# A graph layer with a routed feed-forward: the router's additions, the slots' owners and how the experts get their rows

## The reference, cut to what matters

```python
xn = layernorm(x)
x = x + relu(gcn(xn, edges, W) + b) + mix(xn)          # gcn: sum over edges of h[src] / sqrt(deg[src] deg[dst])
h = layernorm(x)
probs = softmax(h @ gate_w + gate_b)                     # 8 experts
idx = argmax(probs); prb = probs[idx]
pos = (number of earlier nodes with the same idx)
kept = pos < 977
buf[idx, pos] = h where kept
hmid = relu(buf @ w1 + b1)                               # 977 x 256 x 1024 per expert
ybuf = hmid @ w2 + b2                                    # 977 x 1024 x 256 per expert
x = x + nan_to_num(ybuf[idx, min(pos, 976)] * (prb * kept))   # nan -> 0, +-inf -> +-10000
```

## Time and profile before

| | us |
|---|---|
| median of three runs | 3071.05 (3069.43 to 3091.04) |
| the profiled execution, its own time | 3054.78 |
| its span, first to last instruction | 3053.0 |
| `prepare` | 0 to 166.5 |
| `aggregate_and_mix` | 166.5 to 2515.6 |
| `route` | 2515.6 to 2633.2 |
| `experts` | 2633.2 to 3053.0 |

### The profile page before, as it was taken

How to read it: one execution, slowest core, us unless ns; L and a number is a source line. 1 busy time by engine, 2 the same in 40 slices (tenths; PEclk the granted TensorE clock), 3 DMA queues, 4 the chain that set the end, 5 groups by cost and what they waited for, 6 DMA issues and landing times. The chain is left out here.

```text
span 3053.0 us, 35559 instructions
## 1 busy us (share of the span) xinstructions
PE 1786.6 (59%) x8925; PEld 1543.9 (51%) x8925; DVE 1245.6 (41%) x3349; ACT 813.4 (27%) x1591; POOL 1787.7 (59%) x1892
## 2 busy tenths in 40 slices
PE   2746556646555555655555555556433336599997
PEld 2634444445455444554455444545432335488986
DVE  3522222223333433433434334343322229478885
ACT  1312122212222222222232222222200006445452
POOL 6046556666666666666666666666666654244545
PEclk6878788866666666666666676666566565699998
DMA  5367766666666666666666655666566653322120
GB/s 172 141 198 220 213 201 190 178 187 185 185 186 184 176 180 185 178 174 177 179 186 188 181 172 171 182 181 177 170 188 183 181 164 121 119 68 96 57 97 11
DMA packets 194891, 502.10 MB, mean 164 GB/s; under 512 B 35250, under 2 KB 76225, under 8 KB 194586
## 3 DMA queue, kind: packets, MB, share of 16 engines
q0 software_dynamic: 132160, 423.59, 47.8%
q1 hardware_dynamic: 62554, 76.36, 7.6%
HBM read 461.89 MB, written 41.92 MB: 165 GB/s over the span
## 5 line engine op out<-in xcount | busy, mean ns | idle before, releaser
L767 POOL DMA_INDIRECT ring<-node_rows,src_chunk x1563 | 1486.3, 951 | 920.2 <-issue 434.2
L805 PE MATMUL p_item<-ring,sel 128*128 x3512 | 847.0, 393 | 647.6 <-DVE acc L1051 371.8
L805 PEld LDWEIGHTS p_item<-ring,sel 128*128 128x128 f32 x3512 | 690.9, 275 | 747.3 <-issue 744.8
L1051 DVE TENSOR_TENSOR acc<-acc,p_item 128x256 f32 (+1 forms) x439 | 183.6, 418 | 628.2 <-remote 495.0
L1033 DVE SCALAR_TENSOR_TENSOR sel<-dst_chunk,nbase,p_col 128x512 fp32r<-128x512 f32 x439 | 325.7, 742 | 62.3 <-issue 50.8
L845 PE MATMUL p_g<-x1T,w1t_sb 128*128 128x128 f32 x392 | 100.5, 437 | 206.6 <-ACT x1T L958 171.5
L845 PEld LDWEIGHTS p_g<-x1T,w1t_sb 128*128 128x128 f32 x392 | 86.3, 324 | 220.4 <-ACT x1T L958 181.9
L1056 DVE SCALAR_TENSOR_TENSOR kf<-p_q,ke 128x256 f32<-128x256 f32 x49 | 20.8, 425 | 404.3 <-ACT ke L991 348.7
L1561 POOL TENSOR_TENSOR low<-low,big 128x256 f32<-128x256 f32 x64 | 56.6, 885 | 172.5 <-DVE big L1741 172.0
L1675 PE MATMUL e_y<-w2h,hTh 128*128 128x256 f32 x512 | 148.8, 291 | 2.2 <-DVE hTl L1727 1.6
L1675 PE MATMUL e_y<-w2h,hTl 128*128 128x256 f32 x512 | 143.0, 279 | 0.0
(11 more groups left out here) (242 smaller groups left out, 3165.1 us busy)
## 6 DMA issues: line engine op xcount, KB each, us to landing
ring<-node_rows,src_chunk POOLq DMA_INDIRECT x1563
self_rows<-node_rows SPq DMA_DIRECT2D x49, 256.0 KB
node_rows<-halves SPq DMA_DIRECT2D x11, 1024.0 KB, 4.3
w1raw<-in_w SPq DMA_DIRECT2D x8, 1024.0 KB, 7.0
w2raw<-in_w SPq DMA_DIRECT2D x8, 1024.0 KB, 6.0
expert_rows<-empty SPq DMA_DIRECT2D x61, 130.0 KB
rows<-expert_rows SPq DMA_DIRECT2D x8, 910.0 KB
res<-in_x SPq DMA_DIRECT2D x7, 896.0 KB, 7.4
```

The lines of the kernel that those rows point to most:

```text
L767: nc.gpsimd.indirect_dma_start(ring[:, c % RING // U, c % U, :], None, table, bass.IndirectOffsetOnAxis(src_chunk[:, c:c + 1], 0)).then_in ...
L805: mm = pe.matmul(p_item[i % PSLOT][:, 0:C], sel[:, i % SELR, u, :], rows[:, u, h * C:(h + 1) * C].bitcast(F32R), start=(u == 0 and h == 0) ...
L1051: nc.vector.tensor_tensor(a, a, p_item[j % PSLOT][:, 0:C], ALU.add).then_inc(added, 1)
```

## The change

In `aggregate_and_mix` the writes of zeros are gone. The block's bias is now added when the node's own row is copied into `acc`, multiplied by `sqd` = sqrt(deg), and three operations at the end of the mixing work take the factor `sqd` as well, so that `acc` and `res` have one scale; the number of operations stays as it was, the three and the copy being other forms. `sqd` is one more operation at the end of `prepare`.

In `route` one addition per block is left in `x2`. PE transposes the rows as they are, the gate's weights are centred once instead, and the logits are scaled. The groups are 12, 12, 12, 8 and 5 blocks, and the small operations stand among the blocks of the next group. Instead of a row number for a scatter, each node gets a slot number, split into `slot_lo` (0 to 127) and `slot_hi` (0 to 63). DVE makes one-hot matrices of them (`one_hi`, `one_lo`, `node_of`), and PE sums them over all nodes to the node of each slot (`owners`). SP writes the rows with their columns to `node_features`; ACT multiplies the rows by `dinv` for the output.

In `experts` POOL gathers an expert's rows from `node_features` with eight indirect DMAs of 128 rows: those of experts 0 and 1 at the start, those of expert e+2 behind the last store of expert e. POOL's addition of `rows` is gone; DVE adds them behind its choice of finite numbers, and `total` is gone. Before its addition DVE waits until the store of the tile before the last has read `oo`. ACT waits for all eight gathers of an expert, for the first expert tile by tile.

```diff
-SLOTS = EXP * CAP
-NFILL = -(-SLOTS // P)
...
-RGR = 7
-NOUT = NBLK // RGR
+RB = [0, 12, 24, 36, 44, NBLK]
+RGM = 12
+NOUT = 2 * (len(RB) - 1)
...
-                if k >= 20 and k % 4 == 0 and (k - 20) // 4 < NFILL:
-                    lo = (k - 20) // 4 * P
-                    rows = min(P, SLOTS - lo)
-                    sp.dma_start(slots[lo:lo + rows, :], empty[0:rows, :]).then_inc(dma_empty, 16)
...
-                nc.vector.tensor_copy(acc[:, b, 0:C], p_self).then_inc(self_out, 1)
+                nc.vector.scalar_tensor_tensor(acc[:, b, 0:C], g["bias_b"]["gb"][:], sqd[:, b:b + 1], p_self,
+                                               ALU.mult, ALU.add).then_inc(self_out, 1)
...
-                    nc.vector.tensor_tensor(yn[:], yn[:], g["bias_b"]["ln2g"][:], ALU.mult).then_inc(fin, 1)
+                    nc.vector.scalar_tensor_tensor(yn[:], yn[:], sqd[:, b:b + 1], g["bias_b"]["ln2g"][:], ALU.mult,
+                                                   ALU.mult).then_inc(fin, 1)
...
-                    V.scalar_tensor_tensor(acc[:, b, 0:C], acc[:, b, 0:C], dinv[:, b:b + 1], g["bias_b"]["gb"][:],
-                                           ALU.mult, ALU.add).then_inc(s1, 1)
-                for b in range(gi * GR, gi * GR + GR):
-                    v.wait_ge(s1, b + 1)
-                    V.scalar_tensor_tensor(acc[:, b, 0:C], acc[:, b, 0:C], 0.0, res[:, b, :], ALU.max, ALU.add
-                                           ).then_inc(s2, 1)
...
+            def x2(b):
+
+                V.scalar_tensor_tensor(acc[:, b, 0:C], acc[:, b, 0:C], 0.0, res[:, b, :], ALU.max, ALU.add
+                                       ).then_inc(x2_ok, 1)
+
+            def stats(gi, b):
+                v.wait_ge(x2_ok, b + 1)
+                chain(V.bn_stats(stt[:, gi % 2, b - RB[gi], :], acc[:, b, 0:C]))
...
+                if i == 2:
+                    chained()
+                    chain(V.scalar_tensor_tensor(slot[:, 0:k], m2[:, 0:k], float(RT * P), place[:, 0:k], ALU.mult,
+                                                 ALU.add))
+                    chain(V.scalar_tensor_tensor(kept_lo[:, 0:k], place[:, 0:k], float(CAP), node_lo[:, w], ALU.is_lt,
+                                                 ALU.mult))
+                    chain(V.scalar_tensor_tensor(kept_hi[:, 0:k], place[:, 0:k], float(CAP), node_hi[:, w], ALU.is_lt,
+                                                 ALU.mult))
+                if i == 3:
+                    chained()
+                    chain(V.tensor_scalar(slot_lo[:, 0:k], slot[:, 0:k], P - 1, None, ALU.bitwise_and))
+                    chain(V.tensor_scalar(slot_hi[:, 0:k], slot[:, 0:k], 7, None, ALU.arith_shift_right))
+                if i == 4:
+                    chained()
+                    wait(v, mapped, gi - 1)
+                    chain(V.tensor_tensor(one_hi[:, 0:k, :], counts(k, NS), over(slot_hi[:, 0:k], k, NS),
+                                          ALU.is_equal))
+                if i == 5:
+                    V.tensor_tensor(one_lo[:, q, 0:k, :], counts(k, P), over(slot_lo[:, 0:k], k, P), ALU.is_equal
+                                    ).then_inc(one_ok, 1)
+                if i == 6:
+                    chained()
+                    V.tensor_tensor(node_of[:, q, 0:k, 0, :], one_hi[:, 0:k, :], over(kept_lo[:, 0:k], k, NS),
+                                    ALU.mult).then_inc(one_ok, 1)
+                if i == 7:
+                    V.tensor_tensor(node_of[:, q, 0:k, 1, :], one_hi[:, 0:k, :], over(kept_hi[:, 0:k], k, NS),
+                                    ALU.mult).then_inc(one_ok, 1)
...
+            for gi in range(NG):
+                for u in range(size(gi)):
+                    b = RB[gi] + u
+                    x2(b)
+                    if gi > 0:
+                        steps(gi - 1, 2 * u, 2 * size(gi))
+                    if u > 0:
+                        stats(gi, b - 1)
+                    if gi > 0:
+                        steps(gi - 1, 2 * u + 1, 2 * size(gi))
...
+            v.wait_ge(mapped, NG)
+            chain(V.tensor_copy(low_part[:], p_map[:, 0:NS]))
+            chained()
+            chain(V.scalar_tensor_tensor(node_f[:], p_map[:, NS:2 * NS], float(P), low_part[:], ALU.mult, ALU.add))
+            chained()
+            V.tensor_scalar(slot_row[:], node_f[:], -1.0, 0.0, ALU.add, ALU.max).then_inc(dv, 1)
+            V.tensor_scalar(gone[:], node_f[:], 0.0, float(NOWHERE), ALU.is_equal, ALU.mult).then_inc(dv, 1)
+            v.wait_ge(dv, n[0] + 2)
+            V.scalar_tensor_tensor(slot_node[:], node_f[:], -1.0, gone[:], ALU.add, ALU.add).then_inc(dv, 1)
...
+                for b in blocks_of(t):
+                    s.wait_ge(x2_ok, b + 1)
+                    nc.scalar.activation(res[:, b, :], acc[:, b, 0:C], ACT.Copy, scale=dinv[:, b:b + 1]
+                                         ).then_inc(scaled, 1)
...
+            def transposes(t):
+                t_.wait_ge(x2_ok, blocks_of(t)[-1] + 1)
+                wait(t_, xT_ok, t - 1)
+                for b in blocks_of(t):
+                    for a in range(CH):
+                        mm = pe.transpose(p_t[t % 2][:, b % 2 * CH + a, :], acc[:, b, a * P:(a + 1) * P], ident[:])
+                mm.then_inc(tr_ok, 1)
...
+                for b in range(RB[gi], RB[gi + 1]):
+                    u = b - RB[gi]
+                    mm = pe.matmul(p_map[:, 0:2 * NS], one_lo[:, q, u, :],
+                                   node_of[:, q, u].rearrange("p a m -> p (a m)"), start=(b == 0),
+                                   stop=(b == NBLK - 1))
...
-        def load_rows(sp, e, u):
-            sp.dma_start(rows[:, u, 0:RT - 1, :],
-                         slots[bass.ds(e * CAP, (RT - 1) * P), :].rearrange("(t p) c -> p t c", p=P)
-                         ).then_inc(d_r[u], 16)
-            sp.dma_start(rows[0:LASTR, u, RT - 1, :], slots[bass.ds(e * CAP + (RT - 1) * P, LASTR), :]
-                         ).then_inc(d_r[u], 16)
...
+            def load_rows(e):
+
+                for t in range(RT):
+                    r, k = nrows(t), e * RT + t
+                    nc.gpsimd.indirect_dma_start(
+                        rows[0:r, e % 2, t, :], None, feats, bass.IndirectOffsetOnAxis(slot_row[0:r, k:k + 1], 0)
+                        ).then_inc(gathered[t] if e == 0 else d_r[e % 2], 16)
+
+            load_rows(0)
...
+            def store(e, t):
+                r, k = nrows(t), e * RT + t
+                pool.wait_ge(o_ok, 2 * k + 2)
+                nc.gpsimd.indirect_dma_start(
+                    out, bass.IndirectOffsetOnAxis(slot_node[0:r, k:k + 1], 0), oo[0:r, t % 2, :], None,
+                    bounds_check=N - 1, oob_is_err=False).then_inc(sent[t % 2], 16)
...
+            for e in range(EXP):
...
-                    wait_apart(pool, inf_ok, T * 2 + 2, dma_out, 16 * NOUT)
+                    pool.wait_ge(inf_ok, (e * RT + t) * 2 + 2)
                     nc.gpsimd.tensor_tensor(low[0:r, t % 2, :], low[0:r, t % 2, :], big[0:r, t % 2, :], ALU.add
                                             ).then_inc(pool_st, 1)
-                    pool.wait_ge(pool_st, T * 2 + 1)
-                    wait(pool, sent[t % 2], (e * (RT // 2) + t // 2) * 16)
-                    nc.gpsimd.tensor_tensor(oo[0:r, t % 2, :], low[0:r, t % 2, :], rows[0:r, u, t, 0:C], ALU.add
-                                            ).then_inc(pool_st, 1)
                     if t > 0:
-                        store(t - 1)
-                store(RT - 1)
-
-            all_experts(pool, expert)
+                        store(e, t - 1)
+                store(e, RT - 1)
+                if e + 2 < EXP:
+                    load_rows(e + 2)
...
-                V.copy_predicated(oo[0:r, t % 2, :], finite[0:r, t % 2, :], total[0:r, t % 2, :]
-                                  ).then_inc(o_ok, 1)
+                V.copy_predicated(low[0:r, t % 2, :], finite[0:r, t % 2, :], yv[0:r, t % 2, :]).then_inc(o_ok, 1)
+                wait_apart(v, o_ok, 2 * T + 1, dma_fb, 16)
+                wait_apart(v, sent[t % 2], (e * (RT // 2) + t // 2) * 16, dma_fb, 16)
+                V.scalar_tensor_tensor(oo[0:r, t % 2, :], rows[0:r, u, t, 0:C], rows[0:r, u, t, C + 3:C + 4],
+                                       low[0:r, t % 2, :], ALU.mult, ALU.add).then_inc(o_ok, 1)
```

More of the change, by code:

```diff
@@ new lines, in route @@
+    NG = len(RB) - 1
+    NS = EXP * RT
+    GAPS = 2 * RGM
+    XT = 3
+    assert all(b % 2 == 0 for b in RB[:-1]) and max(b - a for a, b in zip(RB, RB[1:])) == RGM
+    with ExitStack() as st:
+        stt = sb("stt", [P, 2, RGM, 6], st=st)
+        mvg = sb("mvg", [P, 2, RGM, 2], st=st)
+        sdg = sb("sdg", [P, 2, RGM], st=st)
+        veps = sb("veps", [P, 2, RGM], st=st)
+        tmp = sb("tmp_r", [P, RGM], st=st)
+        deg2 = sb("deg2", [P, NBLK], st=st)
+        xT = sb("xT_r", [P, XT, 2 * CH, P], st=st)
@@ L1345, in _ @@
[L1345 to L1356 removed]
```

(20 more changed lines are left out.)

520 lines of the change are left out of this document (290 added, 230 removed).

## The result

The changed kernel takes 3118.45 us (median of four runs, 3111.62 to 3120.42) where the kernel before takes 3080.94 (four runs, 3069.43 to 3091.04). The ratio is 1.0119, with a 95% interval of 1.0068 to 1.017: some 37 us slower. The forecast was 3078, 0.2% slower, with a range from 3040 to 3106. It started from a median of 3071.05 for the kernel before; the four runs here have 3080.94, so 10 of the 40 us between 3078 and 3118.45 are not the change's.

The account below looks back on a forecast made before the run. Four successive stages were judged separately, DVE setting the router's pace and POOL's gathers delaying PE. 0 - 21 + 0.5 + 34 - 7 = +6.5 on the profiled 3054.8 gives 3061.3, and 16.3 to the median makes 3078; range 3040 to 3106.

Parts of the forecast that it names:

- The graph stage: Gathers' stage: removing the writes of zeros and changing DVE's forms gives 0, with 15 us allowed to both sides.
- rival 4: Gathers' stage: the change alters the 420 us of waits, moving it 30 us or more either way; chance 0.08.
- The router: Router stage: DVE sets the pace; blocks -13, head +1.4, end -9, in sum -21 us.
- The one-hots: Router: DVE's new one-hot matrices, 320 numbers per block, take 0.36 us per block.
- The end: Router's end, from the last group's statistics: 18 us instead of 27.3, which is -9.
- The start: Start of the experts: eight gathers and landing put layer 1's first product at 15.6 us instead of 15.1, +0.5.
- The rows of the later experts: Six fetches during layer 1: eight gathers behind the last store make xe late, 5.7 us each, +34 us.
- rival 3: Later experts: the last store isn't earlier, 10.3 us late per expert, 62 in all, total +34.5, 3106; chance 0.08.
- the landing: Later experts' fetch: the last gather's rows land 2 us after its end, so xe starts 5.5 us later.
- the restart: Later experts: PE's slower clock after its idle time adds 0.2 us per expert.
- Layer 2 and the tail: Experts' layer 2 and end: POOL without oo keeps up with PE, tail -5, transpose waits -2, together -7 us.
- rival 2: Later experts: DVE's two-input operations block POOL's gathers fully, 8 us late each, total +20.5, 3092; chance 0.15.

Follow-up runs that it names:

- zeros_back: Changed kernel with the graph stage's 61 writes of zeros put back, to a table nobody reads: 3109.45 us, ratio 1.0164 to the kernel before.
- best: Changed kernel, gather waits tile by tile, second-weight loads behind the gathers: 3055.23 us, ratio 0.9995 to the kernel before; on another chip 2623.59 us, 0.9928.
- before: The kernel before the change, unedited: 3080.94 us, median of four runs.
- after: The changed kernel, unedited: 3118.45 us, ratio 1.0119 to the kernel before.
- tilewise: Changed kernel, but ACT waits for each tile's gather apart instead of for all eight: 3060.47 us, ratio 1.0001 to the kernel before.
- no_refetch: Changed kernel without fetches for experts 2 to 7, which reuse the rows of experts 0 and 1 (results wrong): 2626.51 us, ratio 0.992 to the kernel before.
- before_ctl: Kernel before with two graph-stage waits on loaded numbers written as max(number, 0): 2650.67 us, ratio 1.0006 to the kernel before.

## Why the prediction was wrong

The terms behind the graph stage sum to +34.5 by the first two profiles, where +6.5 were said. That is 28 of the 40 us; 10 are the median that the forecast started from, and 3 are left.

**The graph stage (0, give or take 15)** was right on four of the five chips: where it can be told to a few us, it is 1.5 and 2.4 us longer. On the chip of `zeros_back` and `best` it may be longer by 17 to 24, which would be a part of rival 4; no profile of the kernel before shows it. The zeros cost nothing, as the earlier trace rows said.

**The router (-21)** was -15.4. DVE's work among the blocks fell as counted (81.9 to 70.3 us busy, -12, where -13 was said), but the stretch from the first addition to the last statistics stayed at 88 us. The step that failed is that DVE sets the pace by its work alone. DVE waits for 16.7 us in that stretch, in the kernel before for 3.6:

```profile
DVE acc L1333 <- ACT sdg L1506: 6.0, 4, 4.1
DVE psum_e L1397 <- ACT ex L1511: 4.0, 2, 3.4
DVE cur L1408 <- PE r_in L1576: 2.5, 1, 2.5
DVE cur L1408 <- PE r_in L1580: 2.3, 1, 2.3
DVE acc L1460 <- POOL node_hi L1262: 1.9, 1, 1.9
```

The reason, as far as the order on the engines tells it: a group's small steps stand among the next group's blocks, and on ACT and PE the root, the exponent and the places stand among the copies and products of those blocks, so DVE waits for these too (PE is busy for 69.4 us of that stretch, 56.9 before). No run takes this apart. The one-hots were priced well (0.96, 1.75, 0.96 and 0.95 us for 12 blocks, 0.385 per block for 0.36). The end, in turn, was better than said by 5 us, and this luck hides half of the miss among the blocks: from the last statistics to `slot_node` 9.1 us, where 14.5 were said, and 3.6 for the last writes and the meeting.

**The start (+0.5)** was +4.2. The forecast counted the gathers' issue and took 2.5 us of landing from stores; the first gather's rows took 6.0, beside 3 MB of weights and biases, and 2.2 us of it went when 2 MB of them waited. Yet the first `xe` isn't late: it starts 7.7 us after the stage's beginning, 8.4 in the kernel before. What is longer is the way from it to the first product of layer 1, 11.6 us instead of 6.7:

```profile
2655.51 1.09 ACT L1759 ACTIVATE xe<-rows 128x256 f32<-128x256 f32 x2 [14.54 <-DMA rows<-node_features,slot_row]
...
2660.38 0.60 ACT L1759 ACTIVATE xe<-rows 128x256 f32<-128x256 f32 x1
2660.88 0.35 ACT L1767 CAST bTh<-e_t 128x256 fp32r<-128x256 f32 x1
2661.14 0.62 ACT L1772 CAST w1h<-w1raw 128x512 fp32r<-128x512 f32 x1
2661.66 0.60 ACT L1759 ACTIVATE xe<-rows 128x256 f32<-128x256 f32 x1
...
2667.06 0.74 PE L1837 MATMUL e_f<-bTh,w1h 128*128 128x490 f32 x1 [1.66 <-issue]
```

ACT makes the four parts of `w1h` between the tiles now, one tile every 1.27 us without a wait; in the kernel before they were done ahead of the first `xe`. The forecast had the last `xe` at 13, behind the gathers; it is at 16.4, behind ACT's own work. No run moves these four.

**The rows of the later experts (+34)** were +53 (from one S to the next it is 57.2 us on average in the six, 48.4 in the kernel before), the term that made the forecast wrong. The mechanism was the one forecast. The last gather was said to be out at S + 24.8 and was at S + 24.2 to 25.0. That is luck, two errors that cancel: the last store ends at S + 13.4 on average (13.7 in the expert shown) instead of 11.8, since DVE's choice for tile 7 still stands behind two columns (rival 3; it is 1.6 earlier than in the kernel before, where 2.7 were said), and the gathers take 1.11 us on average and not 1.5. What was mis-sized stands behind the last gather:
- the landing: 2 us were taken from the stores, it was 2.8 to 5.6, 4.4 on average, of which 1.6 are the second weights' load. `xe` was 7.0 us later than before (mean of six: 29.1 against 22.1) where 5.5 were said; that is 9 us in six experts (the forecast also took 21.3 for before, the earliest of the six).
- the restart: 0.2 us were put down for PE's clock. It is 1.8: from the first transposes to the next S it takes 27.4 us instead of 25.6 (means of six). That is 10 us in six. The clock accounts for nearly all of it: behind the stop the granted clock is 0.50, and 13 to 23 products, 18 on average, take 0.41 us and follow each other after 0.21, where at 1.00 they take 0.28 and follow after 0.11 to 0.12. In the 14 us behind a stop PE has no other gap, so DVE's last `hTh` and `hTl`, late behind `xe`, hold up nothing. Behind the stop and 8 us later (the clock is the third number from the end):

```profile
2860.30:2864.00 3.70, 3.70 (x18) 3.70 (x19) 2.19 (x3) 1.74 (x4) 0.00 (x0) 0.50 0.02 4
2868.00:2872.00 4.00, 4.00 (x36) 4.00 (x36) 1.58 (x6) 1.79 (x4) 0.74 (x1) 1.00 0.01 2
```

```profile
2861.21 0.41 PE L1850 MATMUL e_y<-w2h,hTl 128*128 128x256 f32 x1
2861.42 0.41 PE L1850 MATMUL e_y<-w2h,hTh 128*128 128x256 f32 x1
```

and in the kernel before, at the same place:

```profile
2866.04 0.28 PE L1675 MATMUL e_y<-w2h,hTl 128*128 128x256 f32 x1
2866.15 0.28 PE L1675 MATMUL e_y<-w2h,hTh 128*128 128x256 f32 x1
```

**Layer 2 and the tail (-7)** were about right, the tail by luck. The layers without any wait for rows are 377.6, 7 to 10 us under the kernel before, some 6 of which are that kernel's own gaps of 0.7 to 1.9 us ahead of the next expert's first transposes. The tail is 6 to 7 shorter, where 5 were said, but 2.6 of this is an operation that the forecast didn't have: POOL's DRAIN, with which POOL ends its part of each function. The three lines are from `before`, `after` and `tilewise`:

```profile
L1447 POOLq DRAIN  x1: 5280/5280/5280, 3047.5 to 3047.5; - x1
L1625 POOLq DRAIN  x1: 2670/2670/2670, 3114.5 to 3114.5; - x1
L1625 POOLq DRAIN  x1: 9203/9203/9203, 3048.2 to 3048.2; - x1
```

It takes 5.28 us in every version of the kernel before, 2.67 in every version of the changed one with one wait for eight, 6.59 in `no_refetch` and 9.20 in `tilewise` and both `best`, whatever the chip. That is why the tail of `tilewise` is 18.8, although its last store starts 7.0 us after PE's end as against 8.9 in the changed kernel, and PE's last expert takes 44.3 us in both. What makes the DRAIN long stays open. The prediction's 5.8 us from the last scatter of the router to its end, put down to landing, hold a DRAIN of 4.05 as well.

**The rivals.** A complete block of POOL by DVE (rival 2) is against the rows: the gather at 2850.09 took 0.94 us with `w2l`, an operation with two inputs, beside it for 0.70. Some gathers do take 1.47, and `hTh` took 0.79 instead of 0.66 beside gathers, so the two engines do hold each other up, by a part of an operation. The gather at 2851.33 took 1.00 with `hTl` beside it from 2851.56 on, and `hTl` its usual 1.18. The Trainium skill, "SBUF — State Buffer", "SBUF: two separate sides", says that the one of the two that starts first keeps the shared ports for its whole operation and the other stands still. For a VectorE operation with two inputs it says so only against a GpSimd operation that reads SBUF, a condition that the prediction left out; whether a gather, which reads its row numbers there, is one, it doesn't say. If it is, the trace doesn't agree for these gathers: the one at 2850.09 should have ended after 2850.81 + 0.9, or `w2l` after 2851.03, and neither did.

The price came out between rivals 2 and 3: 8.8 us per fetch against the kernel before (7.0 + 1.8), where they had 8 and 10.3, but by another way than theirs. (By its own terms rival 3 is 9.9 late, 59 in all, 3103; the 10.3 and 3106 there are added up too high, and with them the end of the range.)

## What to carry to other kernels

When one transfer becomes several small ones, give each its own wait: the same 48 gathers at the same places cost 59 us of the layers with one wait for eight and nothing with a wait for each (49 of the whole, as the tail grew by 6). When a fetch is on the path that sets the end, its price is not only its length but also the landing behind the last transfer, 4.4 us here, and the slow first products of a PE that has stood still, 1.8 us here. And a load with some 43 us to spare (the second weights are asked for at 2850.84 and first read at 2894.18) belongs behind the one that has none, even if its queue is another.

## What the runs showed of the hardware

The same kernel took 3081, 3057 and 3088 us on three chips and 2650 and 2646 on two others. On the four of these that have a profile of it the layers of the experts are equal (385 to 388 us); the graph stage takes 2350 to 2386 on the first kind and 1976 on the second, with POOL's gathers 1.26 us apart on average (1976/1563); `prepare` takes 166 to 170 and 129 to 133. What the first kind adds shows as POOL's 420 us of waits for free places in the ring, of which `before_ctl` has 14.7. What is slower there stays open. A change that is judged on one chip of the first kind alone carries some 15 us of uncertainty: the 52 and the 25 us above are each clear of the other.
